# Unit 0's first state group in a two-way Mamba tower: spread by TensorE products in place of a round trip through HBM

## The chip, the core and the metric

The kernel runs on one core of a Trainium2 chip. Its engines are TensorE (PE; its weight loads are PEld), VectorE (DVE), ScalarE (ACT), GpSimd (POOL) and SyncE (SP, which here only issues DMAs); each takes its instructions in program order, and they wait for each other through semaphores. The metric is the time of one execution on the device, in microseconds (us); lower is better.

## The reference

4096 tokens (2 sequences of 2048) are looked up in an embedding table (64 columns of it), normalised, and passed through a Mamba block that runs forward and backward over each sequence, and then through a layer in which each token picks one of 32 experts. The part that matters here is the scan:

```python
def step(h, inp):
    u_t, dt_t, B_t, C_t = inp
    dA = jnp.exp(dt_t[..., None] * A)
    h = h * dA + (dt_t * u_t)[..., None] * B_t[:, None, :]
    y = jnp.einsum('bdn,bn->bd', h, C_t)
...
xz = u @ in_w.T
x, z = jnp.split(xz, 2, axis=-1)
x = silu(dwconv_causal(x, conv_w, conv_b))
x_dbl = x @ xproj_w.T
dt = jax.nn.softplus(x_dbl[..., :R] @ dt_w.T + dt_b)
```

There are 128 channels d and 16 states n for each channel, so each time step has 2048 state rows.

## The kernel before

**Units.** The two sequences, each in four chunks of 512 tokens and in both directions, make 16 units (`u`). Units 0 to 3 are the forward direction of the first sequence, chunk by chunk. A unit's 2048 state rows are 4 groups `r` by 4 quarters `q` of 128 partitions x 512 steps. For each (r, q), numbered p = 4r + q in a unit, ACT makes the decay exp(dt A) into one of PSUM's banks 0 to 2 (`decay`, L1094) and DVE scans it over the input (`scan`, L1529). The input dt*u*B of a whole group is one product of 128x2048, on DVE (`input_product`, L1514) or on POOL (L482). POOL multiplies by C (`by_c`, L491), and TensorE folds the states into channels (`sum_states`).

**How dt and du reach the state rows.** dt and du = dt*x are 128 channels x 512. A quarter's 128 state rows are 32 channels repeated 4 times. So dt and du are stored to HBM (`dt_dram`, `du_dram`) and read back with the repetition as `dtS` and `duS`; in unit 0 in two halves of two quarters (`first_half`), and the first group's input is made half by half (`first_product`, L1668).

**Softplus of unit 0.** ACT computes relu and abs of the product `pre` (+ bias), exp, plus one, and log; DVE adds what rounding lost (`log1p_error`, L1437) and sums up (`first_softplus`). Units 1 and on sum on TensorE (`sum_dt`, L657 to L659) and copy out (`dt_out`).

**Work around unit 0.** While unit 0 starts, the pipeline of the next chunks runs through all engines: DVE normalises (`begin_norm`, `norm_var`, `norm_newton`, `start_u2`, `start_residual`), TensorE transposes (`turn_chunk`, L589), ACT copies into `uT` (L1031), TensorE makes the first convolution (`x_chunk`, L605), ACT applies silu (L1037), TensorE the second convolution (`conv`, L630), and ACT silu again (`conv_silu`, L1049). Unit n needs conv(n). ACT keeps silu and exp/ln in two table sets, so that each group of silus stands between two table loads (L994, L991); below such a group is called a burst. In unit 0 the bursts stand at fixed places among the decays (`first_unit(p)` on ACT), and `softplus_in(2)` stands behind the last.

**What sets the order.** The order on every engine is written out by hand, and every engine has a list of its own for unit 0; `first_unit(p)` on ACT and on DVE says what comes behind decay p or scan p. From unit 1 on, the lists are loops over units. PSUM's banks are named: `Y`, `SHORT`, `PRE`, `ZED`, `LONG` are banks 3 to 7.

## Time and profile before

| | us |
|---|---|
| three runs: median (lowest, highest) | 557.37 (554.32, 560.18) |
| the profiled execution, its own time | 554.74 |
| its span on the core | 552.9 |
| DVE, PE, POOL, ACT busy in the span | 481.8, 463.2, 474.9, 376.7 |

All times in the rows are measured from the span's start. The profiled execution is 2.63 us faster than the median of the three runs, and 1.84 us of its time lie outside the span. Its mean granted TensorE clock is 0.935 of full speed.

### The profile page before, as it was taken

The numbers are of one execution on the slowest core, as the hardware profiler recorded it, in microseconds if no ns is written. First come the engines' busy times: TensorE is split into PE (matmuls) and PEld (weight loads), VectorE is DVE, ScalarE is ACT, GpSimd is POOL, SyncE is SP. The second block draws the span as 40 slices with busy tenths as digits, with TensorE's granted clock in tenths as the row PEclk, the third lists the DMA queues.
The fourth block names the chain that finished last, engine by engine and source line by source line (L and its number), as shares of the span: only waits on it lengthen the run. The fifth ranks groups of instructions, "written<-read, shape, count | busy, mean of one in ns | idle before, by whom it ended". The sixth has DMA issues, their size and how long they took to land.

```text
span 552.9 us, 5695 instructions
## 1 busy us (share of the span) xinstructions
PE 463.2 (84%) x1653; PEld 180.2 (33%) x1653; DVE 481.8 (87%) x591; ACT 376.7 (68%) x666; POOL 474.9 (86%) x157
## 2 busy tenths in 40 slices
PE   2977968878799797979898889888988987795987
PEld 1422322323233332324233424342334332332343
DVE  2675985989898998999989989999999999999951
ACT  2488685686867786777858497869785885364643
POOL 5552799998989999899999998999999999999800
PEclk9999989999989897989799799999998997796999
DMA  4149795958392936648384839293949395830000
GB/s 58 16 61 213 157 200 124 209 143 178 95 206 70 199 97 155 155 113 181 100 168 138 182 114 195 85 207 103 198 112 202 98 196 123 188 60 9 0 11 19
DMA packets 51008, 71.05 MB, mean 129 GB/s; under 512 B 16498, under 2 KB 17442, under 8 KB 50978
## 3 DMA queue, kind: packets, MB, share of 16 engines
q1 hardware_dynamic: 47986, 69.36, 55.3%
q0 software_dynamic: 1024, 1.05, 2.7%
q10 hardware_dynamic: 1968, 0.29, 0.3%
q8 instruction: 13, 0.21, 0.2%
q14 instruction: 17, 0.14, 0.1%
HBM read 60.19 MB, written 10.49 MB: 128 GB/s over the span
## 4 chain that ended last, share of the span: by engine, by line
DVE 38%; PE 37%; issue 10%; ACT 7%; POOL 3%; DMA 2%; SPq 2%; DVEq 0%; ACTq 0%
DVE st L1529 21%; DVE st L1514 8%; PE ps L630 5%; PE ps L729 3%; PE ps L717 3%; PE ps L692 3%; PE ps L811 2%; POOL st L491 2%; PE ps L657 2%; PE ps L700 2%; PE ps L705 2%; ACT ps L1094 2%; PE ps L669 1%; PE ps L745 1%; DVE zr L1535 1%
## 5 line engine op out<-in xcount | busy, mean ns | idle before, releaser
L491 POOL TENSOR_TENSOR st<-st,repC 128x2048 f32<-128x2048 f32 x63 | 285.2, 4529 | 20.0 <-ACT carry L1100 14.4
L1529 DVE TENSOR_TENSOR_SCAN st<-ps,carry,st 128x512 f32<-128x512 f32 x192 | 235.1, 1267 | 4.7 <-ACT ps L1094 3.8
L1094 ACT ACTIVATE ps<-dtS,negA 128x512 f32<-128x512 f32 x256 | 170.8, 681 | 48.3 <-DVE st L1529 47.3
L482 POOL TENSOR_TENSOR st<-duS,repB 128x2048 f32<-128x2048 f32 x30 | 135.9, 4530 | 0.5 <-DMA duS<-du_dram 0.5
L1529 DVE TENSOR_TENSOR_SCAN st<-ps,zero,st 128x512 f32<-128x512 f32 x64 | 78.8, 1269 | 5.3 <-ACT ps L1094 4.9
L717 PE MATMUL ps<-st,fold 128*32 128x512 f32 x504 | 69.6, 625 | 12.8 <-POOL st L491 12.8
L1514 DVE TENSOR_TENSOR st<-duS,ps 128x2048 f32<-128x2048 f32 x33 | 74.9, 2270 | 0.2 <-issue 0.2
L630 PE MATMUL ps<-act,wT 128*128 128x512 f32 x128 | 57.8, 593 | 0.3 <-ACT act L1037 0.3
L463 POOL DMA_INDIRECT x<-in_L_tok_ple_table,idx x32 | 31.0, 968 | 29.4 <-DMA dtS<-dt_dram 13.0
L692 PE MATMUL ps<-xr,Bw 128*128 128x512 f32 x68 | 38.2, 645 | 7.9 <-ACT bc_sb L1086 6.2
L669 PE MATMUL ps<-xr,wT 128*32 128x512 f32 x32 | 20.4, 725 | 22.3 <-DVE st L1514 22.3
L705 PE MATMUL ps<-Bw,nought 128*128 128x512 f32 x68 | 35.6, 610 | 0.0
L811 PE MATMUL ps<-xfT,w 97*128 97x512 f32 x64 | 34.9, 642 | 0.8 <-ACT tall L1134 0.5
L630 PEld LDWEIGHTS ps<-act,wT 128*128 128x128 f32 x128 | 23.8, 189 | 29.2 <-issue 27.8
L717 PEld LDWEIGHTS ps<-st,fold 128*32 128x32 f32 x504 | 10.0, 109 | 59.0 <-issue 31.2
L1134 ACT ACTIVATE tall<-ps,b 128x512 f32<-128x512 f32 x32 | 21.4, 676 | 11.0 <-PE ps L811 11.0
L991 ACT ACT_TABLE_LOAD x17 | 21.8, 1283 | 9.7 <-issue 9.5
L729 PE MATMUL ps<-zr,wT 128*128 128x512 f32 x32 | 20.4, 723 | 9.1 <-DVE zr L1535 9.1
L1100 ACT ACTIVATE carry<-st 128x4 f32<-128x4 f32 x48 | 9.9, 206 | 24.8 <-DVE st L1529 24.5
L657 PE MATMUL ps<-l_,ident 128*128 128x512 f32 x30 | 22.9, 856 | 2.1 <-DVE e_ L1437 2.1
L692 PEld LDWEIGHTS ps<-xr,Bw 128*128 128x128 f32 x68 | 11.9, 196 | 28.5 <-issue 20.2
L700 PE MATMUL ps<-xr,skip 128*128 128x512 f32 x32 | 19.7, 701 | 0.0
(141 smaller groups left out, 634.0 us busy)
## 6 DMA issues: line engine op xcount, KB each, us to landing
repC<-bc_dram SPq DMA_DIRECT2D x64, 256.0 KB, 10.4
duS<-du_dram SPq DMA_DIRECT2D x60, 256.0 KB, 4.4
dtS<-dt_dram SPq DMA_DIRECT2D x60, 256.0 KB, 7.4
repB<-bc_dram SPq DMA_DIRECT2D x60, 128.0 KB, 3.0
dt_dram<-dt SPq DMA_DIRECT2D x16, 256.0 KB, 3.2
du_dram<-du SPq DMA_DIRECT2D x16, 256.0 KB, 2.0
bc_dram<-bc_sb SPq DMA_DIRECT2D x16, 64.0 KB, 11.1
dtS<-dt_dram SPq DMA_DIRECT2D x8, 128.0 KB, 3.0
```

Of the source, the lines that this page charges most:

```text
L482: pool.tensor_tensor(st[:, r], duS[:, u % 2], row, ALU.mult).then_inc(sem("dbu_pool"), 1)
L491: pool.tensor_tensor(st[:, r], st[:, r], row, ALU.mult).then_inc(sem("hc_ready"), 1)
L630: mm = pe.matmul(ps[:, bank, :], conv_wT(way(u), k), act_at(u, 6 - k if way(u) else k), start=(k == 0), stop=(k == 3))
L657: pe.matmul(ps[:, PRE, :], ident[:], l_[:], start=True, stop=False)
L692: pe.matmul(ps[:, SHORT, :], Bw[:, way(u), r, :], x_of(u), start=True, stop=True) \
L705: pe.matmul(ps[:, Y, :], nought[:], flat(Bw[:, 0]), start=start, stop=False, skip_group_check=True)
L717: mm = pe.matmul(ps[32 * q:32 * q + 32, Y, :], fold[:], st[:, r, q], start=False, stop=(r == NR - 1), skip_group_check=True)
L729: pe.matmul(ps[:, SHORT, :], wT[:, 12 + way(u), :], z_of(u), start=True, stop=True) \
L811: pe.matmul(ps[:, bank, :], w1[:, k, :], xfT_of(u), start=True, stop=True) \
L1094: sc.activation(decay_bank(u, r, q), dtS[:, u % 2, q], ACT.Exp, scale=negA[:, way(u), q, r:r + 1]).then_inc(sem("decay_ready"), 1)
L1514: dve.tensor_tensor(st[:, r], duS[:, u % 2], row, ALU.mult).then_inc(sem("dbu_dve"), 1)
L1529: dve.tensor_tensor_scan(st[:, r, q, order], decay_bank(u, r, q)[:, order], st[:, r, q, order], first, ALU.mult, ALU.add).then_inc(sem("sc ...
```

## The change

Four things change, all in the beginning of the program; the lists from unit 1 on stay as they are.

**Spreading by products.** A selection matrix `sel` (a 128x128 block for each quarter, copied from the identity) stands in the staging area. TensorE multiplies it with dt and with du (`spread_dt`, `spread_du`), one product of 128x512 for each quarter, into PSUM. ACT's first four decays read dt there (`first_decay`), in the bank that they also write. B's row is copied out of PSUM to `ga` once, and DVE's first four input products (`first_product`, now one quarter each) read du in PSUM and B in `ga`. The round trip through HBM remains, and groups 1 to 3 of unit 0 still read it.

**Softplus shared.** In unit 0, DVE computes the relu and the plus one; ACT computes abs, exp and log.

**TensorE's list.** `b_rows(0, 0)` and the eight spreads are put in front of and between chunk 1's work; `b_rows` move up by one place each, `gate_chunk(0)` moves down behind `x_chunk(2)`; two of three filler products (`add_nought`) go; chunk 1's convolutions use bank `PRE`.

**Lists of ACT, DVE and POOL.** DVE's normalisation of chunks 2 and 3 is moved in among the first four scans. On ACT, `squares`, `bc_out`, softplus(1) and the bursts move: the first from behind decay 6 to behind decay 8, with the gate's silu in it, the second from behind decay 11 to behind decay 12. POOL's eight gathers wait for du's store in place of dt's load; `dt_times_x(1)` stands behind `by_c(0, 0)` in place of ahead of it.

TensorE, from the products behind conv(0) on. xr, wT L669 is `bc(0)`, L692 `b_rows(0, 0)`, L618 `gate_chunk(0)`, L605 `x_chunk(1)`, L630 `conv(1)`. Before:

```order
L669 MATMUL ps<-xr,wT 32x512
L711 MATMUL ps<-nought 128x512 x2
L589 MATMUL ps<-ident,u2d 128x128 x4
L618 MATMUL ps<-tall,gate_wT 128x512
L692 MATMUL ps<-xr,Bw 128x512
L605 MATMUL ps<-tall,wT 128x512 x2
L589 MATMUL ps<-ident,u2d 128x128 x4
L630 MATMUL ps<-act,wT 128x512 x4
```

Now, where L851 and L862 are the spreads of dt and du, L697 is `b_rows`, L610 `x_chunk(1)` and L635 `conv(1)`:

```order
L674 MATMUL ps<-xr,wT 32x512
L716 MATMUL ps<-nought 128x512 x2
L697 MATMUL ps<-xr,Bw 128x512
L851 MATMUL ps<-dt,st 128x512
L862 MATMUL ps<-du,st 128x512
L851 MATMUL ps<-dt,st 128x512
L862 MATMUL ps<-du,st 128x512
L593 MATMUL ps<-ident,u2d 128x128 x4
L851 MATMUL ps<-dt,st 128x512 x2
L862 MATMUL ps<-du,st 128x512
L610 MATMUL ps<-tall,wT 128x512 x2
L593 MATMUL ps<-ident,u2d 128x128 x4
L862 MATMUL ps<-du,st 128x512
L635 MATMUL ps<-act,wT 128x512 x4
```

Six spreads stand ahead of `x_chunk(1)` and one more ahead of `conv(1)`; `gate_chunk(0)` has left this stretch.

ACT in unit 0, from decay 6 (the first row) over both bursts to what stands behind the second. L1094 are decays, L994 and L991 the table loads, L1100 is `keep_last`. Before:

```order
L1094 ACTIVATE ps<-dtS,negA 128x512
L994 ACT_TABLE_LOAD
L1037 ACTIVATE act<-ps,conv_b 128x512 x2
L991 ACT_TABLE_LOAD
L1094 ACTIVATE ps<-dtS,negA 128x512 x3
L1100 ACTIVATE carry<-st 128x4
L1094 ACTIVATE ps<-dtS,negA 128x512 x2
L994 ACT_TABLE_LOAD
L1049 ACTIVATE xr<-ps,conv_b 128x512
L1056 ACTIVATE zr<-ps 128x512
L1049 ACTIVATE xr<-ps,conv_b 128x512
L991 ACT_TABLE_LOAD
L1094 ACTIVATE ps<-dtS,negA 128x512 x2
```

Now, from decays 7 and 8 (the first row) on; L1128 are decays, L1028 and L1025 the table loads, L1134 is `keep_last`, L1115 `dt_out(1)`, L1096 the begin of `softplus_in(2)`:

```order
L1128 ACTIVATE ps<-dtS,negA 128x512 x2
L1115 ACTIVATE dt<-ps 128x512
L1028 ACT_TABLE_LOAD
L1071 ACTIVATE act<-ps,conv_b 128x512
L1076 ACTIVATE gate<-ps 128x512
L1071 ACTIVATE act<-ps,conv_b 128x512
L1025 ACT_TABLE_LOAD
L1134 ACTIVATE carry<-st 128x4
L1128 ACTIVATE ps<-dtS,negA 128x512 x4
L1028 ACT_TABLE_LOAD
L1083 ACTIVATE xr<-ps,conv_b 128x512
L1090 ACTIVATE zr<-ps 128x512
L1083 ACTIVATE xr<-ps,conv_b 128x512
```

Decays 7 and 8 now stand ahead of the first burst, which holds one silu more, and four decays (9 to 12) between the two bursts in place of five (7 to 11). Behind the second burst two decays (12 and 13) stood ahead of `softplus_in(2)`; now none does.

The diff, cut to what the words and the steps below speak of:

```diff
                     dt_times_x(2)
                 if u == 0:
-                    pool.wait_ge(sem("dt_first_1"), 64)
+                    pool.wait_ge(sem("du_in_dram"), 16)
                     for t in range(TB + 4, TB + 12):
                         gather(t)
-                    dt_times_x(1)
                 if 2 in on_pool(u):
                     input_product(u, 2)
                 by_c(u, 0)
+                if u == 0:
+                    pool.wait_ge(sem("du_spread"), NQ)
+                    dt_times_x(1)
                 by_c(u, 1)
...
@@ -595,7 +599,8 @@
                 if n == 0:
                     pe.wait_ge(sem("wT_copied"), 7)
                 if n == 1:
-                    pe.wait_ge(sem("x_ready"), 1)
+                    pe.wait_ge(sem("abs_first"), 1)
+                    pe.wait_ge(sem("sp_a"), 2)
...
+            def spread_dt(q):
+
+                pe.wait_ge(sem("dt_ready"), 1)
+                if q == 0:
+                    pe.wait_ge(sem("sel_ready"), 1)
+                    pe.wait_ge(sem("dtproj_ready"), 2)
+                if q == NQ - 1:
+                    pe.wait_ge(sem("scanned"), 1)
+                pe.matmul(ps[:, q % 3, :], sel[:, q], dt[:], start=True, stop=True).then_inc(sem("dt_spread"), 1)
+
+            def spread_du(q):
+
+                pe.wait_ge(sem("du_ready"), 1)
+                if q >= 2:
+                    pe.wait_ge(sem("dbu_first"), q - 1)
+                elif q:
+                    pe.wait_ge(sem("b_first"), 1)
+                else:
+                    pe.wait_ge(sem("wT_late"), 1)
+                pe.matmul(ps[:, SHORT if q % 2 else Y, :], sel[:, q], du[:], start=True, stop=True).then_inc(sem("du_spread"), 1)
+
...
+            b_rows(0, 0)
+            spread_dt(0)
+            spread_du(0)
+            spread_dt(1)
+            spread_du(1)
             turn_chunk(1)
-            gate_chunk(0, 0)
-            b_rows(0, 0)
-            x_chunk(1, 1)
+            spread_dt(2)
+            spread_dt(3)
+            spread_du(2)
+            x_chunk(1, PRE)
             turn_chunk(2)
-            conv(1, 2)
+            spread_du(3)
+            conv(1, PRE)
+            b_rows(0, 1)
             pre(1)
             bc(1)
             skip_product(0)
-            add_nought(3)
+            add_nought(1)
             turn_chunk(3)
-            b_rows(0, 1)
+            b_rows(0, 2)
             sum_dt(1)
             x_chunk(2, LONG)
-            b_rows(0, 2)
+            gate_chunk(0, PRE)
+            b_rows(0, 3)
             x_chunk(3, ZED)
             conv(2, PRE)
-            b_rows(0, 3)
             sum_states(0, 0)
             zed(0, ZED, 0)
...
+            sc.wait_ge(sem("pre_ps"), 1)
+            sc.activation(e_[:], ps[:, PRE, :], ACT.Abs, bias=dt_b[:, 0:1]).then_inc(sem("abs_first"), 1)
+            sc.wait_ge(sem("abs_first"), 1)
+            sc.activation(e_[:], e_[:], ACT.Exp, scale=-1.0).then_inc(sem("sp_e"), 1)
+            sc.wait_ge(sem("sp_w"), 1)
+            sc.activation(l_[:], dt[:], ACT.Ln).then_inc(sem("sp_l"), 1)
+            bc_out(0)
             squares(2)
             rsqrt(1)
-            softplus_in(0)
-            softplus_exp(0)
-            softplus_plus1(0)
-            softplus_ln(0)
+            sc.wait_ge(sem("b_ps"), 1)
+            sc.activation(ga[:], ps[:, SHORT, :], ACT.Copy).then_inc(sem("b_first"), 1)
+            sc.wait_ge(sem("rates_ready"), 1)
+
+            def first_decay(q):
+
+                sc.wait_ge(sem("dt_spread"), q + 1)
+                sc.activation(decay_bank(0, 0, q), ps[:, q % 3, :], ACT.Exp, scale=negA[:, 0, q, 0:1]) \
+                  .then_inc(sem("decay_ready"), 1)
+
+            first_decay(0)
+            first_decay(1)
+            uT_chunk(1)
             rsqrt(2)
-            bc_out(0)
-            decay_rates(1)
-            uT_chunk(1)
+            first_decay(2)
+            first_decay(3)
             silu_tables()
-            gate_silu(0, 0)
-            act_silu(1, 1)
+            act_silu(1, PRE)
             uT_chunk(2)
             squares(3)
-            conv_silu(1, 2)
+            conv_silu(1, PRE)
             exp_ln_tables()
             rsqrt(3)
-            sc.wait_ge(sem("rates_ready"), 1)
+            keep_last(0, 0)
+            softplus_in(1)
+            bc_out(1)
+            softplus_exp(1)
...
-                if p == 1:
-                    softplus_in(1)
-                    bc_out(1)
-                if p == 2:
-                    softplus_exp(1)
+                if p == 4:
                     softplus_plus1(1)
-                if p == 3:
                     softplus_ln(1)
+                if p == 5:
                     uT_chunk(3)
-                if p == 5:
-                    keep_last(0, 0)
+                if p == 6:
+                    decay_rates(1)
+                if p == 8:
                     dt_out(1)
-                if p == 6:
+                if p == 8:
                     silu_tables()
                     act_silu(2, LONG)
+                    gate_silu(0, PRE)
                     act_silu(3, ZED)
                     exp_ln_tables()
-                if p == 9:
                     keep_last(0, 1)
-                if p == 11:
+                if p == 12:
                     silu_tables()
                     conv_silu(2, PRE)
                     z_silu(0, ZED)
                     conv_silu(3, LONG)
                     exp_ln_tables()
-                if p == 13:
                     keep_last(0, 2)
                     softplus_in(2)
...
-                log1p_error(0)
+                dve.wait_ge(sem("sp_e"), 1)
+                dve.tensor_scalar(dt[:], e_[:], 1.0, None, ALU.add).then_inc(sem("sp_w"), 1)
+                dve.wait_ge(sem("sp_w"), 1)
+                dve.scalar_tensor_tensor(e_[:], dt[:], -1.0, e_[:], ALU.add, ALU.subtract).then_inc(sem("sp_c"), 1)
                 dve.wait_ge(sem("sp_c"), 1)
-                dve.tensor_tensor(l_[:], l_[:], e_[:], ALU.subtract).then_inc(sem("sp_log1p"), 1)
+                dve.tensor_tensor(v_[:], v_[:], e_[:], ALU.subtract).then_inc(sem("sp_log1p"), 1)
                 dve.wait_ge(sem("sp_log1p"), 1)
-                dve.tensor_tensor(dt[:], v_[:], l_[:], ALU.add).then_inc(sem("dt_ready"), 1)
+                dve.wait_ge(sem("sp_l"), 1)
+                dve.tensor_tensor(dt[:], l_[:], v_[:], ALU.add).then_inc(sem("dt_ready"), 1)
                 dve.wait_ge(sem("dt_ready"), 1)
                 dve.wait_ge(sem("x_ready"), 1)
                 dve.tensor_tensor(du[:], dt[:], x_of(0), ALU.mult).then_inc(sem("du_ready"), 1)
...
+            dve.wait_ge(sem("consts"), 1)
+            ch.mark(dve.tensor_copy(rank[:], ranki[:]))
+            ch.mark(dve.tensor_copy(w1[DM:DM + E], maskf))
+            norm_var(1)
+            ch.mark(dve.memset(xfT[DM:XR], 1.0))
+            begin_norm(2)
+            dve.wait_ge(sem("abs_first"), 1)
+            dve.tensor_scalar(v_[:], ps[:, PRE, :], dt_b[:, 0:1], 0.0, ALU.add, ALU.max).then_inc(sem("sp_a"), 2)
+            dve.wait_ge(sem("sp_a"), 2)
+            first_softplus()
             norm_newton(1)
             start_u2(1)
             start_residual(1)
             norm_var(2)
...
-            def first_product(h):
-
-                two = slice(2 * h, 2 * h + 2)
-                dve.wait_ge(sem(f"du_first_{h}"), 64)
-                dve.wait_ge(sem("b_ps"), dve_nth[0, 0])
-                if h == 0:
+            def first_product(q):
+
+                dve.wait_ge(sem("du_spread"), q + 1)
+                if q == 0:
+                    dve.wait_ge(sem("b_first"), 1)
                     dve.wait_ge(sem("dtproj_ready"), 2)
                     dve.wait_ge(sem("wT_copied"), 9)
-                dve.tensor_tensor(st[:, 0, two], duS[:, 0, two], ps[:, SHORT, :].unsqueeze(1).broadcast_to([P, 2, T]),
-                                  ALU.mult).then_inc(sem("dbu_dve" if h else "dbu_first"), 1)
-                dve.wait_ge(sem("dbu_dve" if h else "dbu_first"), 1)
+                done = ("dbu_first", q + 1) if q < NQ - 1 else ("dbu_dve", 1)
+                dve.tensor_tensor(st[:, 0, q], ps[:, SHORT if q % 2 else Y, :], ga[:], ALU.mult).then_inc(sem(done[0]), 1)
+                dve.wait_ge(sem(done[0]), done[1])
...
                 if p == 0:
+                    norm_newton(2)
+                    start_u2(2)
+                if p == 1:
+                    start_residual(2)
+                    begin_norm(3)
+                if p == 3:
+                    norm_var(3)
                     norm_newton(3)
                     start_u2(3)
-                if p == 2:
+                    input_product(0, 1)
+                if p == 4:
                     log1p_error(1)
                     start_residual(3)
-                if p == 3:
-                    input_product(0, 1)
-                if p == 5:
+                if p == 6:
                     input_product(0, 2)
-                if p == 8:
+                if p == 7:
+                    rates(1)
+                if p == 9:
                     input_product(0, 3)
```

## Rows read from the trace of the kernel before

**Rows 1.** The page's part 4: the engines' shares of the chain that ended last.
```profile
DVE 38%; PE 37%; issue 10%; ACT 7%; POOL 3%; DMA 2%; SPq 2%; DVEq 0%; ACTq 0%
```

**Rows 2.** Chain that ended last, in order of time: start us, length us, what.
```profile
37.63 4.16 DMA dt_dram<-dt
...
48.16 1.23 DVE st L1668
...
56.37 1.13 PE ps L657 x2
...
81.40 2.05 PE ps L692 x2
```

**Rows 3.** Timeline, unit 0's softplus: start, length, instruction, idle before.
```profile
29.51 1.28 ACT L991 ACT_TABLE_LOAD   x1
...
29.54 1.12 PE L651 MATMUL ps<-xr,dtproj 128*128 128x512 f32 x2 [0.78 <-ACT xr L1049]
...
30.80 0.42 ACT L1015 ACTIVATE sq<-xc 128x256 f32<-128x256 f32 x1
...
32.00 0.68 ACT L1063 ACTIVATE e_<-ps,dt_b 128x512 f32<-128x512 f32 x1
...
32.55 0.15 DVE L1413 TENSOR_TENSOR ps<-ps,lnrs 128x8 f32<-128x8 f32 x1
32.71 0.63 ACT L1067 ACTIVATE e_<-e_ 128x512 f32<-128x512 f32 x1
```

**Rows 4.** Timeline, from there to the end of conv(1).
```profile
35.47 0.68 DVE L1437 SCALAR_TENSOR_TENSOR e_<-ps,e_ 128x512 f32<-128x512 f32 x1
...
36.91 0.69 DVE L1453 TENSOR_TENSOR dt<-v_,l_ 128x512 f32<-128x512 f32 x1
...
39.01 1.99 PE L605 MATMUL ps<-tall,wT 128*128 128x512 f32 x4 [1.34 <-ACT tall L1031]
...
41.77 3.70 PE L630 MATMUL ps<-act,wT 128*128 128x512 f32 x8 [0.34 <-ACT act L1037]
...
44.69 0.42 DVE L1505 COPY w<-st 32x512 f32<-32x512 f32 x1
...
45.52 0.69 ACT L1049 ACTIVATE xr<-ps,conv_b 128x512 f32<-128x512 f32 x1 [1.89 <-PE ps L630]
```

**Rows 5.** Timeline, unit 0 from its first scan on.
```profile
49.42 1.28 DVE L1529 TENSOR_TENSOR_SCAN st<-ps,zero,st 128x512 f32<-128x512 f32 x1
...
50.62 0.15 DVE L1413 TENSOR_TENSOR ps<-ps,lnrs 128x8 f32<-128x8 f32 x1
...
51.23 0.88 DVE L1418 SCALAR_TENSOR_TENSOR u2d<-xc,ps 128x256 f32<-128x256 f32 x2
...
55.65 0.67 DVE L1437 SCALAR_TENSOR_TENSOR e_<-ps,e_ 128x512 f32<-128x512 f32 x1
...
58.21 2.26 DVE L1514 TENSOR_TENSOR st<-duS,ps 128x2048 f32<-128x2048 f32 x1
...
60.40 1.28 POOL L475 TENSOR_TENSOR du<-dt,xr 128x512 f32<-128x512 f32 x1
...
60.51 2.46 DVE L1529 TENSOR_TENSOR_SCAN st<-ps,zero,st 128x512 f32<-128x512 f32 x2
...
72.95 4.53 POOL L482 TENSOR_TENSOR st<-duS,repB 128x2048 f32<-128x2048 f32 x1 [0.46 <-DMA duS<-du_dram]
...
73.32 0.69 ACT L1049 ACTIVATE xr<-ps,conv_b 128x512 f32<-128x512 f32 x1 [1.38 <-PE ps L630]
...
76.66 0.66 ACT L1062 ACTIVATE v_<-ps,dt_b 128x512 f32<-128x512 f32 x1
...
80.69 0.57 ACT L1086 ACTIVATE bc_sb<-ps 32x512 f32<-32x512 f32 x1
```

**Rows 6.** TensorE by stretch: from:to length, busy, granted clock, DMA share, GB/s.
```profile
74.80:78.20 3.40, 1.17 (x6) 1.00 1.06 215
...
81.60:85.00 3.40, 3.40 (x5) 0.50 1.10 110
```

More of the change, by code:

```diff
@@ L234, in build @@
         router_w, a = carve(a, DM, rows=E)
-        alog, a = carve(a, 2, NQ, NS)
         idx_f, a = carve(a, P, rows=TILES)
@@ L240, in build @@
         maskf, a = carve(3 * NQ * T, NBLK, P, rows=E)
+        sel, a = carve(a, NQ, P)
+        alog, a = carve(a, 2, NQ, NS)
         assert a <= NR * NQ * T
@@ L610, in gate_chunk @@
                 if n == 0:
-                    pe.wait_ge(sem("wT_copied"), 7)
+                    pe.wait_ge(sem("dt_ready"), 2)
                 elif n == 1:
@@ L624, in conv @@
                     pe.wait_ge(sem("dt_ready"), u)
-                elif u == 1:
-                    pe.wait_ge(sem("dtproj_ready"), 2)
+                    if u == 2:
+                        pe.wait_ge(sem("gate_ready"), 1)
                 elif u == 3:
@@ L698, in skip_product @@
                 else:
-                    pe.wait_ge(sem("wT_late"), 1)
+                    pe.wait_ge(sem("dbu_dve"), dve_nth[u, 0])
                 pe.matmul(ps[:, Y, :], skip[:, way(u), :], x_of(u), start=True, stop=False, skip_group_check=True)
@@ L1088, in decay @@
             def decay(u, r, q):
-                if u == 0 and r == 0:
+                if u == 0 and r == 1:
                     sc.wait_ge(sem(f"dt_first_{q // 2}"), 64)
-                elif r == 0 and q == 0:
+                elif u and r == 0 and q == 0:
                     sc.wait_ge(sem(f"dtS_in_{u % 2}"), spread(u))
@@ L1323, in first_unit @@
                     bc_out(2)
-            for p in range(NR * NQ):
+            for p in range(NQ, NR * NQ):
                 decay(0, p // NQ, p % NQ)
@@ L1370, in _ @@
             dve.memset(uT[:, 0:4], 0.0).then_inc(sem("pads_ready"), 1)
+            dve.wait_ge(sem("ident_ready"), 1)
+            dve.tensor_copy(sel.rearrange("p q (m d) -> p q m d", d=32),
+                            ident[:].rearrange("p (q d) -> p q d", d=32).unsqueeze(2).broadcast_to([P, NQ, 4, 32])) \
+               .then_inc(sem("sel_ready"), 1)
             dve.wait_ge(sem("first_in"), FIRST)
@@ L1485, in _ @@
             begin_norm(1)
-            norm_var(1)
-            begin_norm(2)
             ch.mark(dve.tensor_scalar(minus[:], ident[:], -1.0, None, ALU.mult))
-            ch.mark(dve.memset(xfT[DM:XR], 1.0))
             ch.mark(dve.memset(w1[XR - 1:XR], 0.0))
             ch.mark(dve.memset(router_wT[DM:DM + E, :], 0.0))
+            dve.wait_ge(sem("consts"), 1)
[8 more added lines that the diff above has]
+            first_softplus()
             norm_newton(1)
@@ L1495, in _ @@
             norm_var(2)
-            first_softplus()
-            norm_newton(2)
-            start_u2(2)
-            start_residual(2)
-            begin_norm(3)
-            norm_var(3)
-            rates(1)
-            dve.wait_ge(sem("consts"), 1)
-            ch.mark(dve.tensor_copy(rank[:], ranki[:]))
-            ch.mark(dve.tensor_copy(w1[DM:DM + E], maskf))
-            ch.wait()
             def input_product(u, r):
@@ L1510, in input_product @@
                     dve.wait_ge(sem(f"duS_in_{u % 2}"), spread(u))
+                else:
+                    dve.wait_ge(sem("du_first_0"), 64)
+                    dve.wait_ge(sem("du_first_1"), 64)
                 dve.wait_ge(sem("b_ps"), dve_nth[u, r])
@@ L1689, in _ @@
             for p in range(NR * NQ):
-                if p in (0, 2):
-                    first_product(p // 2)
+                if p < NQ:
+                    first_product(p)
                 scan(0, p // NQ, p % NQ)
```

## The prediction

> **What bounds the kernel now.** I read the shares of the chain first: DVE and TensorE carry it almost evenly, so no single engine is the bound [rows 1]. Then I read the chain in order of time, since the change touches only the beginning. From 37.63 the chain runs through dt's way to HBM and back; the first product of unit 0 starts at 48.16. But 8 us later the chain has left DVE's scans: at 56.37 it is on TensorE, and it reaches unit 1 at 81.40, where TensorE's `b_rows(1, 1)` waits for ACT's `bc_out(2)` [rows 2]. So what ends last before unit 1 is not the scanning of unit 0. It is the preparation of units 1 to 3: convolution, silu, softplus. The timeline gives its stations: `sum_dt(1)` starts when DVE's `log1p_error(1)` (55.65) is done, `conv_silu(3)` stands at 73.32, `softplus_in(2)` at 76.66, `bc_out(2)` at 80.69 [rows 5]. The question is how early the changed kernel reaches these.
>
> **Softplus of unit 0.** The product `pre` ends at 29.54 + 1.12 = 30.66 and ACT's table load at 30.79 [rows 3]. Then: abs 0.68 (to 31.5), DVE's relu at the same price (to 32.2; exp, 0.63, runs beside it), plus one, the rounding error 0.68, and two sums of 0.69 [rows 3, 4]. The log (priced as the exp) hides beside the rounding error. Plus one reads and writes SBUF; no such instruction of this size is in the trace. The nearest rows are a copy of 512 elements in SBUF at 0.42 and an operation that reads PSUM at 0.68 [rows 4]; I take 0.42, as it reads no PSUM, and 0.26 of range. Sum: 32.2 + 0.42 + 0.68 + 0.69 + 0.69, with some 0.1 for the steps between: dt is ready at 34.8, where it was 36.91 + 0.69 = 37.6. That is 2.8 earlier.
>
> **Spreading.** Removed from the path are 48.16 - 37.63 = 10.5 us of round trip [rows 2]. Added are eight products of 128x512. One costs 1.12 us from a standing start, and 0.86 in a row (conv(1), four products, 3.70) [rows 3, 4]. The first two end at about 36.8, and DVE is then still busy: du 0.69 (to 35.5), then chunk 1's and 2's normalisation, which took 32.55 to 35.47 = 2.9 [rows 3, 4]. So the first product (0.68) runs from 38.5 and the first scan from 39.2, against 49.42 [rows 5]: 10.2 us earlier. A decay that reads PSUM in place of SBUF is bounded by 0.63 and 0.69, the extremes of ACT's 128x512 rows [rows 3 to 5], and is hidden anyway.
>
> **What TensorE's order does to chunk 1.** Here the change pays. In order: four spreads from 34.85 (to 38.4), the transposes of chunk 1 (0.5), the fifth spread (39.8). The sixth shares its bank with the first decay and waits for scan 0 (39.2 + 1.28 = 40.5), so it ends at 41.4, the seventh at 42.3, and then the two products of `x_chunk(1)` end at 44.1; before, at 39.01 + 1.99 = 41.0. Behind this stand the transposes and the eighth spread, so that conv(1) starts at 45.3, not at 41.77, and `conv_silu(1)` at 49.0, not at 45.52 [rows 4]. Chunk 1 is 3.5 us later. In the kernel before, this lateness would have been free for 2.6 us, because the first product waited for its DMA until 48.16. Now it stands in DVE's list: silu 0.69 and table load 1.28 (to 51.0), two small ACT operations (0.4), newton and `start_u2(3)` (50.62 to 52.11, so 1.5) and `input_product(0, 1)` 2.26. Scan 4 starts at 49.0 + 6.2 = 55.2, where it started at 60.51: of 10.2 us, 5.3 are left [rows 3, 5].
>
> **The chain that matters.** `log1p_error(1)` stood ahead of scan 4 and now stands behind it: 55.2 + 1.3 = 56.5 against 55.65, 0.85 later [rows 5]. From there TensorE's list up to conv(3) has the same length: `gate_chunk(0)` came in (0.86) and one `b_rows` moved out (0.86). So 73.32 - 56.37 = 16.95 is unchanged, and `conv_silu(3)` starts at 74.2, also 0.85 later [rows 2, 5]. Then silu 0.69, table load 1.28 and a small copy (0.2) lead to `softplus_in(2)` at 76.35. It was 76.66, because two decays stood ahead of it; they are now ahead of the burst or behind [rows 5]. One of them comes back between there and `bc_out(2)`: 76.35 + (80.69 - 76.66) + 0.6 = 81.0, against 80.69. Unit 1 starts **0.3 us later**.
>
> **Where the 5.3 us go.** They turn into two waits of DVE for decays behind ACT's bursts. DVE is through scan 8 at 65.2, but decay 9 stands behind the first burst. That burst needs `x_chunk(3)` (65.1), then silu 0.7 and table load 1.3, so decay 9 is out at 68.0: 2.8 us. Scan 12 ends at 75.2, but decay 13 stands behind `softplus_in(2)`, out at 78.2: 3.0 us.
>
> **A rule about table loads.** In the trace ACT goes on right behind a table load: it ends at 30.79, the next instruction starts at 30.80 [rows 3]. The Trainium skill (ScalarE: Activation LUTs, What ACT_TABLE_LOAD costs) gives 1283 ns for the load and some 1380 ns of drain for each switch. By it, the sum would have one switch more on its path than before, the one behind `conv_silu(1)`, and would end 1.4 us higher. The row decides; the sum has no drain.
>
> **POOL and SP.** POOL's gathers leave the place ahead of `by_c(0, 0)`, and `du` for unit 1 comes behind it; it was made at 60.40, right after dt(1). Now dt(1) is ready some 0.9 us later, and `by_c(0, 0)` (as the other products of POOL, 4.5) has ended by then if C's rows land some 2 us earlier than before, which the earlier loads allow. The next group of POOL waited for du's DMA until 72.95 [rows 5]. I put this at nothing, from -2 to +2. The filler products removed cost nothing, as TensorE waits there. The copy of `sel` (4 x 128 columns, about 0.4 as the copy above [rows 4]) is in DVE's early wait for weights.
>
> **Sum.** From unit 1 on the lists are the same, so a shift of the start passes to the end: +0.3 on the profiled 554.74, that is 555.0. The profiled execution lay 2.63 under the median of the three runs, so the forecast is **557.7 us**: no change. The three runs spread by 1%, so I take 1% (5.6 us) as what this measurement can tell from no change.
>
> **Rival 1: the gain stays.** If unit 1's start hangs on DVE's scans and not on ACT's softplus, then the 5.3 us of scan 4 stay: 557.4 - 5.3 = 552.1. For it speaks that DVE is on 38% of the chain [rows 1]; against it, that at 81.40 TensorE waits for `bc_out(2)` [rows 2], and that both bursts need convolutions which are not earlier. Chance 0.10.
>
> **Rival 2: TensorE falls to half speed in the head.** From 74.8 to 78.2 TensorE was busy for 1.17 of 3.4 us, and then the granted clock was 0.50 (1.2 GHz of 2.4): in 81.6 to 85.0 it is 0.50, and the two passes at 81.40 took 2.05 us, not 1.12 [rows 2, 6]. The new list has TensorE wait for scan 0, for ACT's `uT` and for DVE's products, one after another, between 38 and 50. If the clock drops there, `x_chunk(1)` and conv(1) (5.2 us of products) take up to 3.4 us more, on a path with no slack: 557.7 + 3.4 = 561.1. It decides as soon as one stretch of that part is as empty as the one at 74.8. By my sum TensorE works for over 2 us in each 3.4 us from 35 to 49, which speaks against it. Chance 0.10. The Trainium skill (TensorE: Matmul & The Clock Gate, HAM oscillation) tells of kernels whose clock falls again and again because products wait for data; it speaks for this rival.
>
> **Rival 3: the drop at 78 does not come.** If the last products of unit 0's preparation fall otherwise, `b_rows(1, 1)`, `sum_dt(2)` and `pre(3)` run at full speed. The row's 2.05 against 1.12 is 0.9 for one product [rows 2, 3]; three products more in that stretch could save 0.86 each, less what is after 85.0: about 2 us. 555.7. Chance 0.12.
>
> **Rival 4: POOL is late.** If C's rows land at the old time, du(1) and with it POOL's first group of unit 1 come up to 2 us late: 559.7. Chance 0.08. The forecast itself has 0.60.
>
> **Range and chances.** Rival 1 is the only one near 1% faster, and half of it with some noise lies beyond; rival 2 with noise may pass 1% slower. Faster 0.10, same 0.82, slower 0.08. The range goes from just above rival 1 to rival 2: 553.0 to 561.2; it holds the bounds of plus one and of POOL.
>
> **What the profile will show.** dt ready at 34.8; first scan at 39.2; `conv_silu(1)` at 49; scan 4 at 55.2; `sum_dt(1)` at 57; decay 9 and 13 awaited by DVE for about 3 us each; `bc_out(2)` at 81; from there each unit as long as before. If scan 4 is at 55 and `bc_out(2)` well under 80, the chain through ACT was read wrongly; if `conv_silu(1)` is far over 49, TensorE's clock or its waits were.

## The result

| | before | after |
|---|---|---|
| median of 17 runs each (lowest to highest), us | 554.27 (550.59 to 560.18) | 560.79 (555.08 to 563.60) |
| the profiled execution, us | 554.74 | 558.95 |
| its span; mean granted clock | 552.9; 0.935 | 557.1; 0.926 |

The ratio is **1.0109**, 95% interval 1.008 to 1.0138: 1.1% slower, where I forecast no change (+0.3 us). It is taken from the executions in the fast state alone, so it is not the quotient of the two medians (1.0118). It lies just beyond the 1% that I took as noise.

That 560.79 lies inside my range (553.0 to 561.2) is luck. The range was laid around 557.7, from three runs of the kernel before with a median of 557.37; 17 runs have 554.27. Moved down by these 3.1 us it would be 549.9 to 558.1, and the result lies outside. The kernel became 6.5 us slower by the medians, where 0.3 was forecast.

The page's part 4 of the changed kernel, the engines' shares of the chain [rows 1]:

```profile
PE 34%; POOL 19%; DVE 19%; issue 16%; ACT 5%; DMA 3%; SPq 3%; POOLq 0%; DVEq 0%; ACTq 0%
```

Its chain in order of time: start us, length us, what [rows 2]:

```profile
34.84 3.47 DMA dt_dram<-dt
...
45.81 8.01 DMA duS<-du_dram
53.90 2.30 DVE st L1568
56.22 1.28 DVE st L1583
57.50 0.59 DVE e_ L1488
58.14 1.78 PE ps L662 x2
59.92 1.71 PE ps L663 x2
...
84.65 2.05 PE ps L697 x2
```

dt's way through HBM has not left the chain. It no longer holds the first scan, but now the second group: the last load of du's rows is issued at 45.81 and lands 8.01 us later, and `input_product(0, 1)` starts only then. (That POOL carries 19% of the whole chain, against 3% before, is no mark of the change: two traces of the kernel before with filler products alone, shown below as before_warm and before_best, have 15% and 16%.)

The timeline of the changed kernel, the stations of [rows 4, 5]:

```profile
34.12 0.69 DVE L1508 TENSOR_TENSOR dt<-l_,v_ 128x512 f32<-128x512 f32 x1
...
39.23 1.28 DVE L1583 TENSOR_TENSOR_SCAN st<-ps,zero,st 128x512 f32<-128x512 f32 x1
...
49.10 0.69 ACT L1083 ACTIVATE xr<-ps,conv_b 128x512 f32<-128x512 f32 x1 [2.14 <-PE ps L635]
...
53.90 2.29 DVE L1568 TENSOR_TENSOR st<-duS,ps 128x2048 f32<-128x2048 f32 x1 [0.84 <-DMA duS<-du_dram]
56.22 1.28 DVE L1583 TENSOR_TENSOR_SCAN st<-ps,zero,st 128x512 f32<-128x512 f32 x1
56.24 1.12 PE L697 MATMUL ps<-xr,Bw 128*128 128x512 f32 x2 [1.95 <-DVE st L1568]
58.14 1.78 PE L662 MATMUL ps<-l_,ident 128*128 128x512 f32 x2 [0.78 <-DVE e_ L1488]
59.71 1.91 PE L663 MATMUL ps<-e_,minus 128*128 128x512 f32 x2
61.42 1.26 PE L664 MATMUL ps<-v_,ident 128*128 128x512 f32 x2
...
77.18 0.69 ACT L1083 ACTIVATE xr<-ps,conv_b 128x512 f32<-128x512 f32 x1 [1.60 <-PE ps L635]
79.30 0.67 ACT L1096 ACTIVATE v_<-ps,dt_b 128x512 f32<-128x512 f32 x1
83.94 0.57 ACT L1120 ACTIVATE bc_sb<-ps 32x512 f32<-32x512 f32 x1
```

And TensorE by stretch: from:to length, busy of PE, PEld, DVE, ACT, POOL, then granted clock, DMA share, GB/s [rows 6]:

```profile
55.10:58.50 3.40, 1.49 (x3) 0.59 (x4) 3.33 (x5) 3.32 (x6) 0.52 (x1) 1.00 0.44 107
58.50:61.90 3.40, 3.40 (x5) 1.35 (x4) 3.40 (x4) 2.08 (x6) 3.40 (x1) 0.50 0.56 154
```

Up to `conv_silu(1)` (49.10) every station stands where it was forecast. Then DVE waits 0.84 us for du's rows, TensorE waits 1.95 us for DVE's product and 0.78 for `log1p_error(1)`, is busy for 1.49 of 3.4 us, and falls to half speed (1.2 GHz) just as `sum_dt(1)` begins: its three products take from 58.14 to 62.68, 4.5 us. Before, they took 2.8, from 56.37 [rows 2] to the end of the third:

```profile
58.19 1.02 PE L659 MATMUL ps<-v_,ident 128*128 128x512 f32 x2
```

`bc_out(2)` of the changed kernel starts at 83.94, 3.25 us later than before [rows 5], and unit 1 with it.

### The profile page after: what moved, and what is told of

Read it like the earlier page. It is cut to its first block, busy times and chain, and to the rows that moved or that the text cites. A ratio compares the mean times of both kernels' runs of the same rounds, so it can differ in the third digit from the quotient of the medians.

```text
span 557.1 us, 5741 instructions
## 1 busy us (share of the span) xinstructions
PE 471.1 (85%) x1665; PEld 183.8 (33%) x1665; DVE 484.3 (87%) x596; ACT 376.4 (68%) x665; POOL 474.6 (85%) x157
## 4 chain that ended last, share of the span: by engine, by line
PE 34%; POOL 19%; DVE 19%; issue 16%; ACT 5%; DMA 3%; SPq 3%; POOLq 0%; DVEq 0%; ACTq 0%
POOL st L493 13%; DVE st L1583 10%; POOL st L484 5%; DVE st L1568 4%; PE ps L635 4%; PE ps L816 4%; PE ps L722 3%; PE ps L734 2%; PE ps L662 2%; PE ps L674 2%; PE ps L697 2%; PE ps L663 2%; PE ps L610 2%; DMA duS<-du_dram 1%; PE ps L832 1%
## 5 line engine op out<-in xcount | busy, mean ns | idle before, releaser
L1128 ACT ACTIVATE ps<-dtS,negA 128x512 f32<-128x512 f32 x252 | 168.4, 682 | 48.0 <-DVE st L1583 46.5
L635 PE MATMUL ps<-act,wT 128*128 128x512 f32 x128 | 57.7, 593 | 0.0
L697 PE MATMUL ps<-xr,Bw 128*128 128x512 f32 x68 | 38.3, 647 | 7.2 <-ACT bc_sb L1120 5.3
L816 PE MATMUL ps<-xfT,w 97*128 97x512 f32 x64 | 37.2, 681 | 0.3 <-ACT xfT L1153 0.3
L710 PE MATMUL ps<-Bw,nought 128*128 128x512 f32 x64 | 33.8, 610 | 0.0
L635 PEld LDWEIGHTS ps<-act,wT 128*128 128x128 f32 x128 | 23.9, 190 | 29.1 <-issue 28.0
L1168 ACT ACTIVATE tall<-ps,b 128x512 f32<-128x512 f32 x32 | 21.6, 677 | 11.6 <-PE ps L816 11.5
L1134 ACT ACTIVATE carry<-st 128x4 f32<-128x4 f32 x48 | 9.9, 206 | 22.3 <-DVE st L1583 22.1
L697 PEld LDWEIGHTS ps<-xr,Bw 128*128 128x128 f32 x68 | 11.8, 197 | 28.1 <-issue 22.4
L477 POOL TENSOR_TENSOR du<-dt,xr 128x512 f32<-128x512 f32 x15 | 19.4, 1294 | 0.9 <-ACT dt L1115 0.9
```

Of the source, the lines that this page charges most:

```text
L635: mm = pe.matmul(ps[:, bank, :], conv_wT(way(u), k), act_at(u, 6 - k if way(u) else k), start=(k == 0), stop=(k == 3))
L697: pe.matmul(ps[:, SHORT, :], Bw[:, way(u), r, :], x_of(u), start=True, stop=True) \
L710: pe.matmul(ps[:, Y, :], nought[:], flat(Bw[:, 0]), start=start, stop=False, skip_group_check=True)
L816: pe.matmul(ps[:, bank, :], w1[:, k, :], xfT_of(u), start=True, stop=True) \
L1128: sc.activation(decay_bank(u, r, q), dtS[:, u % 2, q], ACT.Exp, scale=negA[:, way(u), q, r:r + 1]).then_inc(sem("decay_ready"), 1)
```

## The experiments

Ratios are to the kernel before in runs on the same chip; the experiments come from three chips. Changed kernel: 1.0109. A filler is one product of zeros (`add_nought`).

**Fillers back.**

```diff
             skip_product(0)
-            add_nought(1)
+            add_nought(3)
             turn_chunk(3)
```

> The changed kernel with three filler products behind the first product for C again (as in the kernel before) in place of one; nothing else. In the changed kernel's trace TensorE was busy for 1.49 of 3.4 us in 55.1 to 58.5, and then the granted clock was 0.50 from 58.5 to 61.9, over the three products of sum_dt(1), which took from 58.14 to 62.68. Theory A (the emptier TensorE brings the clock down, and this costs the start of unit 1): the two fillers lie in the gap ahead of 56.2, some 0.9 us more work falls into 55.1 to 58.5, sum_dt(1) runs at full speed in 2.9 us, dt_out(1) starts at 61.1, unit 1's first scans come 1.6 us earlier, and the time is 0.3% under the changed kernel's (ratio to the kernel before 1.008). Rival B (the lateness comes from the wait of the input product for du's rows, not from the clock): the start of unit 1 stays where it is, within 0.3 us, ratio 1.011. Rival C: the fillers push the last transposes of chunk 3 back by 1.7 us, the copies into uT behind them end later, and decays 6 and 7 with them; unit 1 is then up to 1 us later, ratio 1.013.

Measured: **1.005** (1.0013 to 1.0087).

**Gathers back.**

```diff
                 if u == 0:
-                    pool.wait_ge(sem("du_in_dram"), 16)
+                    pool.wait_ge(sem("dt_first_1"), 64)
                     for t in range(TB + 4, TB + 12):
```

> The changed kernel with POOL's eight gathers waiting for the second half of dt's rows again, as in the kernel before; nothing else. In the changed kernel the gathers run from 39.9 to 49.6 beside the loads of the first halves of dt's and du's rows, and input_product(0, 1) waited 0.84 us for du's rows, until 53.90. Theory A (the gathers slow the loads): du's rows land by 52.9, the input product starts at 53.1, scan 4 at 55.4, the half-clock stretch over sum_dt(1) may go with it; unit 1 starts 0.8 to 2.5 us earlier, ratio 1.006 to 1.010. Rival B (the loads are slow by themselves): no change in the start of scan 4, ratio 1.011. Rival C (POOL becomes late): the gathers now run from about 47 to 57 and push by_c(0, 0) from 57.98 back only if C's rows land before they end; then sum_states(0, 0) comes later, up to 0.5 us, no more, since POOL waited 8.40 us for C's rows.

Measured: **1.0012** (0.9978 to 1.0047).

**Both back.**

> The changed kernel with both undone: three filler products, and the gathers behind the second half of dt's rows. If the wait for du's rows (0.84 us) and the half clock over sum_dt(1) (1.7 us) are separate causes that add up, unit 1 starts 2.5 us earlier than in the changed kernel, at +0.5 to +1.2 us against the kernel before, as predicted at first, and the ratio is 1.005. If either of them alone brings all, the sum is no better than the better one of the two. If neither is the cause, 1.011.

Measured: **0.999** (0.9964 to 1.0015). By the ratios the gathers undone alone remove most of the loss, and both undone remove all of it. The fillers count for less: their interval just overlaps that of the changed kernel. All three traces are alike in the head: `input_product(0, 1)` does not wait, and from scan 0 to scan 16 (the first of unit 1) it takes 43.5 us, not 46.1 as in the changed kernel. But in all three the first scan came 1.4 to 2.1 us later than in the changed kernel's trace, and `x_chunk(0)`, which took 1.99 us there, took 2.7 to 3.5 us. So the comparison with that trace was not clean. Hence:

**The changed kernel again.**

> The changed kernel, unaltered, for a second trace. In its first trace the conv(0) products of the start ran at full speed, du's rows were awaited for 0.84 us, and the granted clock was 0.50 from 58.5 to 61.9. In the three kernels with one part undone, whose lists are the same up to there, x_chunk(0) ran at half speed (3.48 us for four passes, not 1.99), so that scan 0 came 1.4 to 2.1 us later. Theory A (the order of the changed kernel makes the wait and the drop at sum_dt(1)): both stand in this trace too, and from scan 0 to scan 16 it takes 46.1 us as in the first. Rival B (both were the luck of the first trace, or came from its earlier start): they are gone, and the distance is 43.5 us as in the three kernels with one part undone.

Measured: 554.97 us, mean clock 0.949. Rival B holds for this one execution: no wait, no drop, and 43.5 us from scan 0 to scan 16. The timelines of the start tell the two apart. The changed kernel's first trace:

```profile
21.05 1.13 PE L716 MATMUL ps<-nought 128*128 128x512 f32 x2
22.13 1.99 PE L610 MATMUL ps<-tall,wT 128*128 128x512 f32 x4
```

A late start (the trace of gathers_back; the second trace of the changed kernel has scan 0 at 41.28, 2.05 us later than the first):

```profile
20.86 2.08 PE L716 MATMUL ps<-nought 128*128 128x512 f32 x2
22.73 3.48 PE L610 MATMUL ps<-tall,wT 128*128 128x512 f32 x4
```

So the same program meets an early and a late start. The stretches from 55.1 in the second trace:

```profile
55.10:58.50 3.40, 2.36 (x8) 0.79 (x6) 3.36 (x2) 3.37 (x7) 0.00 (x0) 1.00 0.73 205
58.50:61.90 3.40, 2.65 (x6) 1.25 (x7) 3.37 (x6) 3.23 (x8) 1.98 (x1) 1.00 0.22 66
```

Here too `sum_dt(1)` waited 0.77 us and only one filler stood in the list, and the clock did not fall. So the wait for du's rows is what the first trace had beside it; the missing fillers alone did not bring the drop. The late start loses 2.05 us and gives it back: scan 16 comes at 84.75, against 85.34 in the first trace. Among the 17 runs of the changed kernel the three with a mean clock of 0.943 or more took 555.1 to 556.6 us, the fourteen at 0.923 to 0.934 took 559.0 to 563.6. The wait and the drop are thus not in every execution. In how many they are, the clocks don't tell: half speed over one stretch of 3.4 us lowers the mean of 557 us by 0.003, and the two groups are 0.009 and more apart. Most of that difference lies elsewhere in the program.

**Lateness in the kernel before.** Does a shift of the preparation pass to the end, as the prediction took it?

```diff
                 pe.wait_ge(sem("sp_c"), u + 1)
+                if u == 1:
+                    add_nought(4)
                 pe.matmul(ps[:, PRE, :], ident[:], l_[:], start=True, stop=False)
```

> The kernel before with four filler products between the wait and the products of sum_dt(1): 3.4 us of lateness at that one place, where the predicted chain runs through TensorE. If that chain sets the start of unit 1 and a shift of the start passes on to the end, as the prediction took it: unit 1's scans start 3.4 us later and the time is 3.4 us longer (ratio 1.006). If there is slack behind it (the chain is carried by DVE's scans): unit 1 starts at most 1 us later, ratio 1.002 or less. If lateness in the head also moves the TensorE clock's half-speed stretches in later units for the worse, more than 1.006, with the difference growing after unit 1.

Measured: **1.0063** (1.0019 to 1.0108). The scans of this kernel at the start of unit 1 (16, then 17) and the last pair:

```profile
86.03 1.27 DVE L1531 TENSOR_TENSOR_SCAN st<-ps,carry,st 128x512 f32<-128x512 f32 x1
...
96.27 2.45 DVE L1531 TENSOR_TENSOR_SCAN st<-ps,carry,st 128x512 f32<-128x512 f32 x2
...
526.95 2.45 DVE L1531 TENSOR_TENSOR_SCAN st<-ps,carry,st 128x512 f32<-128x512 f32 x2
```

Before, they stood at 82.08, 92.56 and 523.47: 3.95, 3.71 and 3.48 us. In this trace what `sum_dt(1)` is late, the program is late: `bc_out` of units 2 to 15 is between 3.5 and 4.0 us later throughout. That bears out the chain on which the prediction rested, and speaks against rival 1. (In the changed kernel the lateness did not stay so constant; see the sum below.)

**Warm in the gap ahead of unit 1.** The kernel both_back, and the kernel before, with

```diff
             bc(2)
+            add_nought(5)
             b_rows(1, 1)
```

> The kernel both_back and five filler products (4.3 us) between bc(2) and b_rows(1, 1), where TensorE waited 4.82 us for bc_out(2) (78.6 to 83.4) and then ran at granted clock 0.50 from 82.5 over b_rows(1, 1) and sum_dt(2). Theory A (the idle stretch brings the clock down, and the chain runs over these products): b_rows(1, 1) takes 1.12 us in place of 2.05 and the three products of sum_dt(2) 2.9 us in place of 4.8, so scan 17 comes about 2.7 us earlier, and the ratio falls from 0.999 to 0.994. Rival B (the clock's stretches only move, since something else in unit 1 waits): scan 17 comes less than 1 us earlier, ratio 0.998 or more.

> The kernel before with the same five filler products between bc(2) and b_rows(1, 1), where TensorE waited 5.43 us and b_rows(1, 1) then took 2.05 us at half clock. If the half clock there costs this kernel what the rows say: 0.9 us on b_rows(1, 1) and 0.9 on sum_dt(2), scan 17 comes 1.8 us earlier, ratio 0.997. If it is nothing, 1.000. It also prices how much of a gain of both_back_warm belongs to the fillers alone and would come without the change.

Measured: both_back_warm **1.0045** (1.0005 to 1.0086), before_warm **0.9984** (0.9948 to 1.0021). Locally theory A holds in both. The timeline of both_back_warm:

```profile
77.14 4.56 PE L710 MATMUL ps<-Bw,nought 128*128 128x512 f32 x10
82.03 1.10 PE L697 MATMUL ps<-xr,Bw 128*128 128x512 f32 x2 [0.33 <-ACT bc_sb L1121]
82.97 1.02 PE L662 MATMUL ps<-l_,ident 128*128 128x512 f32 x2
```

`b_rows(1, 1)` takes 1.10 us, not 2.05, and from scan 16 to scan 17 it takes 8.7 us where both_back took 11.6; before_warm has 8.7 for 10.5. The times do not follow: no gain can be told in the kernel before, and both_back_warm lies 0.55% above both_back, each against the kernel before on its own chip. The gain at unit 1 is 1.8 to 2.9 us; I expected it to reach the end and it did not reliably do so.

both_back_warm had the early start (scan 0 at 39.24), so up to unit 1 it is the clean partner of the changed kernel's first trace. Its profiled execution was the slowest of its twelve (562.34 us), and what it lost came behind unit 1: against the next experiment's trace it is 0.1 us later at scan 17 and 8.6 us later at the last pair of scans, with a mean clock of 0.91 from 100 to 550, not 0.94. Its ACT stations:

```profile
74.56 0.69 ACT L1084 ACTIVATE xr<-ps,conv_b 128x512 f32<-128x512 f32 x1 [1.60 <-PE ps L635]
76.67 0.67 ACT L1097 ACTIVATE v_<-ps,dt_b 128x512 f32<-128x512 f32 x1
81.32 0.57 ACT L1121 ACTIVATE bc_sb<-ps 32x512 f32<-32x512 f32 x1
```

The changed kernel has 77.18, 79.30 and 83.94: 2.62 us later from an equal start (the five fillers stand behind this part of TensorE's list). So with the gathers and the fillers undone, the wait and the drop are gone in an early start too. The traces of both_warm_log1p and best_early_start below, early starts with both undone, have neither. For the changed kernel itself there is one trace of an early start, and for either part undone alone there is none.

**log1p_error(1) first.** The kernel both_back_warm, and in DVE's list:

```diff
                     input_product(0, 1)
+                    log1p_error(1)
                 if p == 4:
-                    log1p_error(1)
                     start_residual(3)
```

> The kernel both_back_warm with log1p_error(1) ahead of scan 4 on DVE, as in the kernel before, in place of behind it. The prediction named this order as 0.85 us of lateness. In both_back sum_dt(1) waited 0.33 us for it, behind b_rows(0, 2), and from there TensorE had no gap up to conv(3). If TensorE's list is the chain: sum_dt(1) and all behind it come 0.33 us earlier and no more, while scan 4 comes 0.6 us later; ratio lower by 0.0006, within the noise. If DVE's order counts for all of it: 0.7 to 0.85 us earlier, 0.0015 lower. If scan 4's lateness counts: 0.6 us later.

Measured: **1.0005** (0.9968 to 1.0043). `sum_dt(1)` starts at 56.62, not 57.21, but scan 16 comes only 0.09 us earlier: a little further on `b_rows(0, 3)` waits 0.29 us for DVE, where scan 4 and the next input product are now later. None of the three expectations hit. In the head the order is worth 0.09 us; the lower ratio (1.0005, against 1.0045 for both_back_warm) can't be told from noise.

**Two fillers in the first 14 us**, to make the start the early one:

```diff
             turn(0, 3 * P, router_w).then_inc(sem("wT_ps"), 1)
+            warm(4)
             pe.wait_ge(sem("taps_ready"), 2)
...
             turn(2, 3 * P, dt_w[:, 0]).then_inc(sem("wT_ps"), 1)
+            warm(2)
```

with `warm(n)` a product of `nought` into 128 x 128n of bank `LONG`.

> The changed kernel with two filler products in gaps of TensorE in the first 14 us (128x512 at 8.1, where it was idle for 2.57 us, and 128x256 at 12.5, idle for 1.06). The traces so far have two starts: x_chunk(0) takes 1.99 us and scan 0 comes at 39.2, or it takes 3.48 us (half speed, though the clock row says 1.00) and scan 0 comes at 40.6 to 41.3. In the changed kernel the early start went with the wait for du's rows, the half clock at 58.5 and a span of 557.1, the late one without either and a span of 553.1. Theory A (an early start brings the changed kernel's wait and clock drop): with the fillers TensorE's first rise of speed comes early in every run, scan 0 stands at 39.2 or earlier, the trace shows the half clock over sum_dt(1), and the time stays at the changed kernel's or above, ratio 1.010 to 1.014. Rival B (the early start is a gain of 2 us like any other): ratio 1.006 to 1.008. Rival C (the fillers don't set the first rise): both starts are still met and the ratio is 1.011.

> The kernel gathers_back (POOL's eight gathers behind the second half of dt's rows) with the same two early fillers, so that the start is the early one, in which the changed kernel waited for du's rows. Theory A (the gathers slow the loads of du's rows, the wait of 0.84 us empties TensorE, and its clock falls at sum_dt(1)): input_product(0, 1) does not wait, from scan 0 to scan 4 it takes 16.05 us in place of 16.99, TensorE runs sum_dt(1) in 2.9 us, from scan 0 to scan 16 it takes 43.5 us, and the ratio is 0.999 to 1.003, well below after_early_start. Rival B (the clock at 58.5 falls without the wait too, since one filler is too few): 45.2 us from scan 0 to scan 16, ratio 1.006 to 1.009.

> The kernel both_warm_log1p (three fillers, the gathers back, log1p_error(1) ahead of scan 4, five fillers behind bc(2)) with the same two early fillers. It is the best version of the changed order so far: its trace had the early start (scan 0 at 39.15) and span 551.8, ratio 1.0005. If the late start costs 2.0 us in about half of its runs: ratio 0.999. If the early start always gives what that trace shows: 0.998. If the order of the change has nothing left to give: 1.000 or more, and before_best, the same three additions to the kernel before, stands lower.

> The kernel before with the five fillers behind bc(2) (as before_warm, 0.9984) and the two early fillers. It is what the fillers give without the change. All three traces of the kernel before and its variants had the early start. If their times hide some late starts, ratio 0.997; if the start is always the early one there, 0.998 as before_warm. If fillers in the first 14 us delay the products behind them, up to 0.5 us more.

Measured: after_early_start **1.0089** (1.0052 to 1.0126), gathers_early_start **1.0043** (1.0011 to 1.0075), best_early_start **1.0022** (0.9988 to 1.0055), before_best **0.9971** (0.9934 to 1.0009). Three of the four traces have the late start all the same, that of before_best among them, so rival C holds: these fillers do not set it. The gathers again make half a per cent, 1.0089 against 1.0043, though here the intervals overlap. Their trace pair says nothing on the wait, as both starts were late; after_early_start lost 1.7 us in another way, between conv(1) and `conv_silu(1)`:

```profile
52.63 0.69 ACT L1089 ACTIVATE xr<-ps,conv_b 128x512 f32<-128x512 f32 x1 [3.83 <-issue]
```

ACT waited for nothing that the profile shows; conv(1) had ended at 50.9. What held it stays open. before_best has the lowest ratio of all, and without the change; its interval still holds 1.

## Why the prediction was off, by its own steps

**Softplus and spreading: right.** dt is ready at 34.12 + 0.69 = 34.81 (forecast 34.8), scan 0 starts at 39.23 (39.2).

**Chunk 1: right.** `conv_silu(1)` at 49.10 (49.0). The first scans' gain is eaten by TensorE's list, as worked out.

**Scan 4: the step that failed, first part.** Forecast 55.2, measured 56.22. I had `input_product(0, 1)` start as soon as `start_u2(3)` was done (53.06) and gave du's rows no term at all: I had counted what the gathers' new place means for POOL and not what it means for the loads. In the changed kernel the eight gathers (39.89 to 49.6) run beside the loads of dt's and du's rows (issued from 38.33 to 46.3). The view of du's tile gives the least, median and most that its eight loads take to land. The changed kernel, first trace:

```profile
DMA to landing us min/median/max: 4.1/5.0/8.0
```

both_back_warm, which has the same early start and the gathers back:

```profile
DMA to landing us min/median/max: 4.2/4.7/6.3
```

So in an equal start the gathers add 1.7 us to the slowest load and little to the median. In late starts it is 3.3, 4.6 and 6.5 with the gathers beside the loads (second trace) and 3.1, 3.7 and 4.4 without (gathers_back); the kernel before has 2.8, 3.4 and 4.1. Part of the slowness in the changed order thus has another cause, which stays open. Missing term: 0.84 us.

**From `sum_dt(1)` to conv(3): the step that failed, second part.** "The same length" (16.95 us) holds for the work, not for the clock. From `sum_dt(1)` to `conv_silu(3)` the first trace takes 77.18 - 58.14 = 19.0 us, and in both_back_warm it is 74.56 - 57.21 = 17.35. The missing term is 1.7 us of half speed on three products; the other 0.4 are small steps. I had written that the removed fillers "cost nothing, as TensorE waits there", and had looked at TensorE's time alone, not at its clock. Whether the fillers themselves would have kept the clock up is not shown: the traces without the drop lack the wait for du's rows, with one filler (second trace, gathers_back) as with three. Rival 2 had the mechanism. That its time, 561.1, is near the measured median is luck, from the high base again: it had priced 3.4 us, at two other products, and the medians differ by 6.5. I looked for it between 38 and 50, where TensorE was busy for 9.21 of the 10 us from 39 to 49 and the clock was 1.00, and left out the stretch from 54 to 58, from which the change had taken two fillers and in which its own DVE list put a later product. The Trainium skill's account that was named there (TensorE: Matmul & The Clock Gate, HAM oscillation), products that wait for data and so meet a lower clock again and again, agrees with this trace: behind the 1.95 and 0.78 us of waiting the granted clock was 0.50, and again from 82.4. The rival's chance should have been well above 0.10.

**Behind conv(3): right.** With both parts undone and an early start, `conv_silu(3)`, `softplus_in(2)` and `bc_out(2)` stand at 74.56, 76.67 and 81.32 (forecast 74.2, 76.35, 81.0). DVE waited 3.08 us for decay 13 (forecast 3.0). For decay 9 it waited 1.83 there, 3.52 in both_back and 5.16 in the changed kernel's first trace (forecast 2.8). In both_back_warm another DVE instruction, which makes decay rates (`rates(1)`), took 1.83 us just before, in place of 0.15 to 0.20. The burst is as late as `sum_dt(1)` is, and DVE has nothing to fill the wait with.

**POOL and rival 4: right to be small.** `by_c(0, 0)` moved from 61.63 to 57.98, as C's rows land earlier. `du` for unit 1 is made at 63.44, right after `dt_out(1)`, where it was made at 60.40, and POOL's next group starts at 75.12, 2.17 us later than before. No piece of the chain up to unit 1 runs through either. **Rivals 1 and 3** did not come: `bc_out(2)` is later, not earlier, and the half-speed stretch ahead of unit 1 is there in the changed kernel too (`b_rows(1, 1)` 2.05 us).

**The sum.** Of 3.25 us at `bc_out(2)`, 0.3 was forecast, 0.84 is the wait, 1.7 the clock, and 0.4 small steps. At scan 17 it is 3.72, at the end of this trace 4.2. That looks like a shift which passes to the end, as the prediction took it ("from unit 1 on the lists are the same"), and it is not. `bc_out(7)` is 5.25 us later than before, `bc_out(12)` 1.81, and the last pair of scans 1.48, the changed kernel first:

```profile
524.95 2.45 DVE L1583 TENSOR_TENSOR_SCAN st<-ps,carry,st 128x512 f32<-128x512 f32 x2
```

```profile
523.47 2.45 DVE L1529 TENSOR_TENSOR_SCAN st<-ps,carry,st 128x512 f32<-128x512 f32 x2
```

More than half of the lateness from the head is gone by then in this pair of traces, and the last 2.7 us arise in the tail. both_back does the same: 3.15 us at scan 17, 0.58 at the last pair. The lists are the same, but half speed falls on other stretches of them: the granted clock from 100 to 200, 200 to 300 and 300 to 400 was 0.97, 0.91 and 0.93 before, and 0.93, 0.93 and 0.97 in the changed kernel. So the head accounts for 3.3 us at unit 1, and how much of it is in the 6.5 us by which the medians differ is not shown. What is shown is by the times of the experiments: with the gathers back the loss is nearly gone, with both back it is gone.

How far one program moves by itself shows in the changed kernel's two traces: they are 0.6 us apart at scan 16 and 4.0 us apart at the end. 2.7 us of it arise in the tail, where the first trace's stretch reads

```profile
530.00:541.00 11.00, 9.49 (x25) 5.05 (x26) 5.26 (x16) 3.83 (x9) 0.00 (x0) 0.69 0.00 0
```

and the second's

```profile
530.00:541.00 11.00, 9.33 (x50) 5.19 (x48) 5.38 (x18) 5.04 (x11) 0.00 (x0) 1.00 0.00 0
```

The forecast of "no change" thus failed, as far as the traces show it, on one place: a gap on TensorE, in which a DMA that I had not priced and a clock that I had priced elsewhere met. The rest of the 6.5 us has no shown cause.

## What to carry to other kernels

When work leaves TensorE where it waits, its time is not all that counts: ask for every gap that a change makes longer what runs right behind it, and what that costs at half speed. When a step is moved on a DMA-issuing engine, price the transfers that it will now run beside, not only the queue that it leaves. A gain of 10 us at the first scan was worth nothing, as the chain ran through the preparation of later chunks. Two traces are not enough to follow a few us to the end: compare them at several places, and leave the verdict to the times of many executions. And measure the base of a range well: three runs put this one 3.1 us too high.

## What the runs showed of the hardware

- The start of one and the same program differs from execution to execution: `x_chunk(0)` at 22 takes 1.99 us in seven of the fourteen traces and 2.7 to 3.5 in the others, with the granted clock in the rows at 1.00 in both, and the first scan of the changed kernel comes 2.05 us later in the late one. Two fillers ahead of it did not decide it: three of four traces with them were late.
- An early start need not be a gain: the changed kernel's late start, 2.05 us behind at scan 0, was 0.6 us ahead at scan 16.
- Eight gathers issued by POOL beside the loads of du's rows took the slowest of eight from 6.3 to 8.0 us in an early start and from 4.4 to 6.5 in a late one.
- Five fillers in a gap of 4.8 to 5.4 us took the half speed off the four products behind it, and 1.8 to 2.9 us off the way from scan 16 to scan 17; of that nothing certain was left in the time.
